# The DMAs of the row of maxima, issued by ScalarE in place of SyncE, in a two-layer attention kernel

## The chip, the cores and the metric

The kernel runs on one core of a Trainium2 chip. The metric is the device time of one execution in microseconds (us); lower is better. PE is TensorE, ACT is ScalarE, DVE is VectorE, POOL is GpSimd, SP is SyncE.

## The reference

Two blocks, each attention followed by a feed-forward layer, over x of shape (2, 2048, 256), 16 heads of 16, all in float32:

```
x = x + attn_a(layernorm(x))     # softmax(q k^T / 4, causal), then times a decay matrix of width 512, then v, then W_proj
x = x + ffn(layernorm(x))        # weights are sign(w) times a mean of |w|; gelu between
x = x + attn_b(layernorm(x))     # plain causal softmax attention with biases, and a norm behind it
x = x + ffn(layernorm(x))        # same ffn weights
```

The softmax subtracts the maximum of each query's scores. That maximum is what the change is about.

## The kernel before

The program is a chain of phases: `setup`, then for each of the two layers `projections`, `attention`, `output_projection` and `feed_forward`. `attention` runs twice, as `att_a` (with decay) and as `att_b` (without). In it the 2 × 16 heads are worked off in 8 groups of 4 heads (`GH`), and the 2048 queries of a head in 4 chunks (`c`) of 512 (`CH`).

Each group needs two passes over the scores. The first, items `M` of the plan, computes scores with queries on the partitions (PE, line 841, PSUM tile `pm`) and DVE takes the maximum of each row (lines 776 and 780, tile `mpart`). When a chunk is done (`MF`, `mneg`), PE turns the 16 columns of maxima into rows (`MT`, line 848, tile `px`), and DVE copies them to `mrow` (line 813). The item `MC` then brings `mrow`, 4 DMAs of 2 KB for each chunk, into row 64 (`MROW`) of the query operand `qop`. The second pass, items `S`, computes scores with keys on the partitions (PE, line 867, PSUM tile `ps`). Row 64 of `kop` is one, so the product already has the maximum subtracted, and ACT takes the exponential straight from PSUM (line 739, tile `wt`). The items `PV` and `PO` multiply `wt` with the values (lines 892, 902) and with ones (line 885). In att_a POOL multiplies `wt` by the decay first (line 700, tile `wd`), and for keys that are too far away for the decay table to be non-zero only their share of the sum is needed: ACT takes an exponential in the first pass' own PSUM tile (`FX`, line 746), and the items `FE` (ACT, line 753), `FM` (DVE, line 799), `FT` (PE, line 854) and `FC` (DVE, SP) make a total of them.

`attention_plan` writes down one order of all these items for a step. Every engine walks the same list and does its own part of each item, so the order on an engine's queue is the order of the plan. The first pass runs ahead of the second: in one step of the plan the second pass of group g stands with chunks 2 and 3 of the first pass of group g (d = 0) and chunks 0 and 1 of group g + 1 (d = 1). So a steady step has four `MC` items, the last step has two, and a list ahead of the first step has two. `S` of a chunk starts with a wait of PE for that chunk's `MC` DMAs:

```
if kb == near(c, decayed)[0] and j == 0:
    pe.wait_ge(m_in[c], M_DMAS * (g + 2))
```

PSUM has 4 banks for `pm` and 2 for `ps` in att_a, and 3 and 3 in att_b. PE's n-th `S` waits until ACT's exponential of 2 (or 3) `S` items before is done.

SP's queue has, in the order of the plan, the `MC` DMAs, the DMAs of `FC`, the stores of `y` (`O`), and at the end of a step `load(g + 2)`: 36 DMAs of keys and queries and one of 1 MB of values, 5 MB in all. Before the first step it has both `load(0)` and `load(1)`. SP waits before each `MC` until DVE has written `mrow` (semaphore `x_read`). In the plan `MC` stands between two `S` items, and in chunk 3 of att_a just ahead of `FE`.

Of the kernel before, what the change touches and what calls it, by code (L numbers as in the profile page):

```python
# [9 lines left out]
F32 = mybir.dt.float32  # L10
# [9 lines left out]
CH = 512  # L20
NC = T // CH
TB = CH // P
GH = 4
# [9 lines left out]
MROW = PAIRS * HD  # L33
# [408 lines left out]
def near(c, decayed):  # L442

    return range(TB * max(0, c - 1) if decayed else 0, TB * (c + 1))


def far(c, decayed):

    return range(max(0, c - 1) if decayed else 0)
# [86 lines left out]
def attention(nc, name, decayed, keep, dram):  # L536
# [3 lines left out]
    with ExitStack() as ctx:  # L540
# [4 lines left out]
        qop = sb("qop", [P, 2, GH, T], F32R)  # L545
# [7 lines left out]
        mrow = sb("mrow", [UNITS, NC, P], F32R)  # L553
# [9 lines left out]
        m_in = [sm(f"m_in{c}") for c in range(NC)]  # L563
# [3 lines left out]
        x_written, x_read, mrow_ready = sm("x_written"), sm("x_read"), sm("mrow_ready")  # L567
# [22 lines left out]
        def steps(eng, step):  # L590


            step(-1, -1, 1, FIRST)
            for g in range(GROUPS - 1):
                step(g, g // 2, g % 2, STEP)
            step(GROUPS - 1, GROUPS // 2 - 1, 1, LAST)

        def x_use(g, c, of_sums):

            return X_USES * g + c + sum(f < c for f in FARS) + of_sums  # L600
# [22 lines left out]
        def maxima(g, i, par, d):  # L623

            return (par, i) if d == 0 else (1 - par, i + par)

        @block.sync
        def _(sp):
            for i in range(2):
                sp.sem_inc(y_out[i], 16)  # L630
            for c in range(NC):
                sp.sem_inc(m_in[c], M_DMAS)
            for c in FARS:
                sp.sem_inc(f_out[c], 16)

            def load(g, par, first):
                for c in range(NC):
                    cols = slice(c * CH, (c + 1) * CH)
                    for r in range(PAIRS):
                        rows = slice(r * HD, (r + 1) * HD)  # L640

                        sp.dma_start(kop[rows, par, :, cols].bitcast(F32), qk_g[g, r % 2, 1, :, :, cols]).then_inc(qk_in[par][c], 16)
                        sp.dma_start(qop[rows, par, :, cols].bitcast(F32), qk_g[g, r // 2, 0, :, :, cols]).then_inc(qk_in[par][c], 16)
                    if first:
                        sp.wait_ge(q_padded[par], c + 1)
                    sp.dma_start(qop[MROW:MROW + 1, par, :, cols].bitcast(F32),
                                 qop[96:97, par, :, cols].bitcast(F32)).then_inc(qk_in[par][c], 16)
                sp.dma_start(va[:, par, :, :, :].rearrange("p (c t) j e -> p c (t j e)", c=NC), v_g[g])\
                  .then_inc(v_in[par], 16)

            def step(g, i, par, plan):
                for item in plan:
                    if item[0] == "MC":
                        _, d, c = item
                        mpar, _ = maxima(g, i, par, d)
                        sp.wait_ge(x_read, x_use(g + d, c, 0) + 2)
                        for j in range(GH):
                            sp.dma_start(qop[MROW:MROW + 1, mpar, j, c * CH:(c + 1) * CH].bitcast(F32),
                                         mrow[TB * j:TB * j + TB, c, :].bitcast(F32)).then_inc(m_in[c], 16)
                    if item[0] == "FC":  # L660
                        _, d, c = item
                        sp.wait_ge(x_read, x_use(g + d, c, 1) + 2)
                        sp.dma_start(far_g[g + d, c], frow[:, FARS.index(c), :]).then_inc(f_out[c], 16)
                    if item[0] == "O":
                        c = item[1]
                        sp.wait_ge(o_kept, NC * g + c + 2)
                        sp.dma_start(y_g[g, c], y[:, c % 2, :]).then_inc(y_out[c % 2], 16)
                if plan is STEP and g < GROUPS - 2:

                    sp.wait_ge(e_scores, E_UNITS * (g + 1))  # L670
                    sp.wait_ge(pv_done, KBS * (g + 1) + buffers)
                    load(g + 2, par, False)

            load(0, 0, True)
            load(1, 1, True)
            steps(sp, step)
            for i in range(2):
                sp.wait_ge(y_out[i], 16 * (GROUPS * NC // 2 + 1))
            for c in FARS:
                sp.wait_ge(f_out[c], 16 * (GROUPS + 1))  # L680
# [42 lines left out]
        @block.scalar  # L723
        def _(act):
            act.sem_inc(e_weights, EBANKS)
            act.sem_inc(o_kept, 1)
            act.sem_inc(f_done, MBANKS)

            def step(g, i, par, plan):
                seen = 0  # L730
                for item in plan:
                    if item[0] == "S":
                        _, c, kb, j = item
                        a = P * max(0, kb - TB * c)
                        kq = seen // GH
                        act.wait_ge(e_scores, E_UNITS * g + seen + 1)

                        act.wait_ge(pv_done, KBS * g + kq + 1)
                        act.activation(wt[:, kq % buffers, j, a:CH], pe_[:, seen % EBANKS, 0:CH - a], ACT.Exp)\  # L739
                           .then_inc(e_weights, 1)  # L740
                        seen += 1
                    if item[0] == "FX":
                        _, d, n, c, qb, j, piece = item
                        act.wait_ge(m_reduced, M_UNITS * (g + d) + n + 1 + MBANKS)
                        u = TB * j + qb
                        act.activation(pm[:, n % MBANKS, :], pm[:, n % MBANKS, :], ACT.Exp,  # L746
                                       bias=mpart[:, c, piece, u:u + 1],
                                       accum_out=fsum[:, c, piece, u:u + 1]).then_inc(f_done, 1)
                    if item[0] == "FE":
                        _, d, c = item  # L750
                        act.wait_ge(f_diff, len(FARS) * (g + d) + FARS.index(c) + 1)
                        n = len(far(c, decayed))
                        act.activation(ffactor[:, c, 0:n, :], ffactor[:, c, 0:n, :], ACT.Exp).then_inc(f_factor, 1)
                    if item[0] == "O":
                        c = item[1]
                        act.wait_ge(pv_done, KBS * g + sum(len(near(a, decayed)) for a in range(c + 1)) + buffers)
                        act.wait_ge(y_out[c % 2], 16 * (2 * g + c // 2 + 1))
                        act.activation(y[:, c % 2, :], po[:, :], ACT.Copy).then_inc(o_kept, 1)  # L758

            steps(act, step)  # L760

        @block.vector
# [720 lines left out]
```

## Time and profile before

| what | value |
|---|---|
| three runs | 3030.36, 3037.56, 3042.88 us; median 3037.56 |
| the profiled execution | 3037.05 us, span 3035.3 us |
| busy: PE, DVE, ACT, POOL | 2530.0, 1994.2, 1551.7, 922.8 us |
| mean granted clock of PE | 0.916 of full speed |
| att_a, att_b | from about 164 to 1230 us and from about 1658 to 2725 us of the span |
| SP's queue (q1), ACT's queue (q10) | 223.36 MB and 16.78 MB |

The span is from the first to the last instruction; the time of the execution has 1.75 us around it. "Busy" leaves out waits and also the instructions that issue DMAs. Rows of a timeline give start, duration, engine, line, operation, what is written and read, the count, and in brackets the idle time before and what ended it. A row whose engine is SPq or ACTq is work of that engine's instruction queue.

### The profile page before, as it was taken

Reading aid. Unit: us, or ns where it says so; the run is one execution under the profiler, and the core shown is the slowest. Engines: PE = TensorE matmul, PEld = TensorE weight load, DVE = VectorE, ACT = ScalarE, POOL = GpSimd, SP = SyncE. Lnnn points to the kernel's source line nnn. Section 1 sums busy time; section 2 is a strip of 40 time slices with the busy share of each in tenths; the row PEclk is TensorE's granted clock in tenths of the full one; section 3 lists DMA queues with packets and bytes.
Section 4 is the critical chain, followed back from the end, with each engine's and each line's share of the span. In section 5 each row is a group of like instructions: output and inputs, shape, how many; then the busy total and the mean of one; then the engine's idle time right before and its main releaser. Section 6 shows DMA issues by size and latency. Waiting matters only on the chain. (4 is left out here: it accounts for less than half of the span.)

```text
span 3035.3 us, 45097 instructions
## 1 busy us (share of the span) xinstructions
PE 2530.0 (83%) x14016; PEld 1465.7 (48%) x14016; DVE 1994.2 (66%) x4919; ACT 1551.7 (51%) x3394; POOL 922.8 (30%) x1108
## 2 busy tenths in 40 slices
PE   4847999999999999477975698989889898984498
PEld 3523545455454454356743354545445454533477
DVE  5555777777877775245654686768667686725755
ACT  1206676685776867114421065656556565660144
POOL 0025777777787778200001101011010110112100
PEclk8958999999999999778988599999999999997799
DMA  4992145052350500683269905052350513008632
GB/s 152 268 146 37 23 67 65 25 82 32 55 82 9 82 12 9 105 174 118 84 181 244 121 12 78 8 81 33 56 77 8 81 29 60 12 8 142 151 124 70
DMA packets 195001, 242.97 MB, mean 80 GB/s; under 512 B 25297, under 2 KB 119378, under 8 KB 194002
## 3 DMA queue, kind: packets, MB, share of 16 engines
q1 hardware_dynamic: 177874, 223.36, 39.2%
q10 hardware_dynamic: 16896, 16.78, 1.9%
q8 instruction: 114, 1.87, 0.3%
q14 instruction: 117, 0.96, 0.1%
HBM read 143.99 MB, written 95.03 MB: 79 GB/s over the span
## 5 line engine op out<-in xcount | busy, mean ns | idle before, releaser
L700 POOL TENSOR_TENSOR att_a_wd<-att_a_wt,decay 128x256 f32<-128x256 f32 (+3 forms) x896 | 754.4, 872 | 287.7 <-PE att_a_po L892 139.8
L739 ACT ACTIVATE att_b_wt<-att_b_ps 128x512 f32<-128x512 f32 (+3 forms) x1280 | 597.1, 538 | 443.2 <-PE att_b_ps L867 438.2
L776 DVE TENSOR_REDUCE att_a_mpart<-att_a_pm 128x1 f32<-128x512 f32 x768 | 509.6, 686 | 180.4 <-PE att_a_pm L841 178.4
L776 DVE TENSOR_REDUCE att_b_mpart<-att_b_pm 128x1 f32<-128x512 f32 x768 | 503.4, 686 | 172.3 <-PE att_b_pm L841 171.6
L739 ACT ACTIVATE att_a_wt<-att_a_ps 128x512 f32<-128x512 f32 (+3 forms) x896 | 437.0, 507 | 248.6 <-PE att_a_ps L870 170.7
L841 PE MATMUL att_a_pm<-att_a_kop,att_a_qop 128*128 128x512 f32 (+3 forms) x1280 | 511.0, 422 | 40.1 <-DMA att_a_qop<-att_a_qop 29.0
L867 PE MATMUL att_b_ps<-att_b_qop,att_b_kop 128*128 128x512 f32 (+3 forms) x1280 | 459.6, 389 | 93.9 <-DMA att_b_qop<-att_b_mrow 89.1
L841 PE MATMUL att_b_pm<-att_b_kop,att_b_qop 128*128 128x512 f32 (+3 forms) x1280 | 502.2, 412 | 28.4 <-DMA att_b_qop<-att_b_qop 27.9
L841 PEld LDWEIGHTS att_a_pm<-att_a_kop,att_a_qop 128*128 128x128 f32 x1280 | 239.2, 194 | 289.9 <-DVE att_a_mpart L776 117.4
L841 PEld LDWEIGHTS att_b_pm<-att_b_kop,att_b_qop 128*128 128x128 f32 x1280 | 249.7, 198 | 261.9 <-DVE att_b_mpart L776 107.8
L718 POOL TENSOR_SCALAR_AFFINE_SELECT att_b_wt<-att_b_wt 128x512 f32<-128x512 f32 x128 | 81.3, 635 | 963.1 <-ACT att_b_wt L739 963.1
L867 PE MATMUL att_a_ps<-att_a_qop,att_a_kop 128*128 128x512 f32 (+3 forms) x896 | 330.5, 376 | 37.9 <-DMA att_a_qop<-att_a_mrow 33.8
L867 PEld LDWEIGHTS att_b_ps<-att_b_qop,att_b_kop 128*128 128x128 f32 x1280 | 240.4, 192 | 206.1 <-DMA att_b_qop<-att_b_mrow 91.9
L780 DVE CUSTOM_DVE_ANT_0 att_b_pm<-att_b_pm,late 128x384 f32<-128x384 f32 (+3 forms) x512 | 247.6, 498 | 99.6 <-PE att_b_pm L841 97.4
L902 PE MATMUL att_b_po<-att_b_wt,att_b_va 128*32 128x512 f32 (+3 forms) x2560 | 301.1, 542 | 8.5 <-ACT att_b_y L758 7.8
L746 ACT ACTIVATE att_a_pm<-att_a_pm,att_a_mpart 128x512 f32<-128x512 f32 x384 | 255.1, 666 | 92.6 <-DVE att_a_mpart L776 91.2
L780 DVE CUSTOM_DVE_ANT_0 att_a_pm<-att_a_pm,late 128x384 f32<-128x384 f32 (+3 forms) x512 | 249.5, 497 | 55.6 <-PE att_a_pm L841 54.3
L867 PEld LDWEIGHTS att_a_ps<-att_a_qop,att_a_kop 128*128 128x128 f32 x896 | 169.6, 190 | 119.4 <-ACT att_a_wt L739 51.1
L885 PE MATMUL att_a_po<-att_a_wt,ones_strip 128*32 128x512 f32 (+3 forms) x1792 | 199.1, 513 | 13.6 <-ACT att_a_y L758 13.6
L892 PE MATMUL att_a_po<-att_a_wd,att_a_va 128*32 128x256 f32 (+3 forms) x1792 | 167.1, 445 | 3.7 <-POOL att_a_wd L700 3.7
L1066 PE MATMUL out_b_pp<-out_b_wp,out_b_yn 128*128 128x256 f32 x256 | 72.6, 453 | 68.5 <-DVE out_b_yn L1135 42.9
L1066 PE MATMUL out_a_pp<-out_a_wp,out_a_yn 128*128 128x256 f32 x256 | 78.3, 480 | 59.0 <-DVE out_a_yn L1135 59.0
(189 smaller groups left out, 2632.9 us busy)
## 6 DMA issues: line engine op xcount, KB each, us to landing
att_a_kop<-qk SPq DMA_DIRECT2D x128, 128.0 KB
att_a_qop<-qk SPq DMA_DIRECT2D x128, 128.0 KB
att_b_kop<-qk SPq DMA_DIRECT2D x128, 128.0 KB
att_b_qop<-qk SPq DMA_DIRECT2D x128, 128.0 KB
qk<-qkv_a_qk_hi SPq DMA_DIRECT2D x32, 256.0 KB, 4.9
qk<-qkv_a_qk_lo SPq DMA_DIRECT2D x32, 256.0 KB, 4.3
v<-qkv_a_vt SPq DMA_DIRECT2D x32, 256.0 KB, 4.0
att_a_va<-v SPq DMA_DIRECT2D x8, 1024.0 KB, 22.5
```

The source lines that it names most:

```text
L700: pool.tensor_tensor(wd[:, kq % 2, j, a:z], wt[:, kq % buffers, j, a:z], keep["decay"][:, u:u + z - a], ALU.mult).then_inc(w_decayed, 1)
L718: pool.affine_select(out=block, in_=block, compare_op=ALU.is_ge, fill=0.0, base=0, pattern=[[0, GH], [1, P]], channel_multiplier=-1).then_ ...
L739: act.activation(wt[:, kq % buffers, j, a:CH], pe_[:, seen % EBANKS, 0:CH - a], ACT.Exp)\
L746: act.activation(pm[:, n % MBANKS, :], pm[:, n % MBANKS, :], ACT.Exp, bias=mpart[:, c, piece, u:u + 1], accum_out=fsum[:, c, piece, u:u + ...
L776: dve.tensor_reduce(mpart[:, c, piece, u:u + 1], pm[:, n % MBANKS, 0:w], AX.X, ALU.max, negate=True).then_inc(m_reduced, 1)
L780: dve.tensor_tensor_reduce(out=pm[:, n % MBANKS, 0:w], in0=pm[:, n % MBANKS, 0:w], in1=keep["late"][:, CH - w:CH], scale=-1.0, scalar=-2 * ...
L841: mm = pe.matmul(pm[:, bank, 0:w], qop[:, mpar, j, q0:q0 + P], kop[:, mpar, j, piece * CH:piece * CH + w], start=True, stop=True)
L867: mm = pe.matmul(pe_[:, bank, 0:CH - a], kop[:, par, j, kb * P:(kb + 1) * P], qop[:, par, j, c * CH + a:(c + 1) * CH], start=True, stop=no ...
L885: mm = pe.matmul(po[STRIP * j:STRIP * (j + 1), a:CH], keep["ones_strip"][:, :], wt[:, ones % buffers, j, a:CH], start=first, stop=False)
L892: mm = pe.matmul(po[STRIP * j:STRIP * (j + 1), a:z], va[:, par, kb, j, :], wd[:, kq % 2, j, a:z], start=False, stop=last)
L902: mm = pe.matmul(po[STRIP * j:STRIP * (j + 1), a:CH], va[:, par, kb, j, :], wt[:, kq % buffers, j, a:CH], start=first, stop=last)
L1066: mm = pe.matmul(pp[:, par, t, :], yn[:, par, g, t * P:(t + 1) * P], wp[:, g, :], start=(g == 0), stop=(g == NG - 1))
```

## The change

The four DMAs of `MC`, with the wait for `x_read` ahead of them, go from the list of SP to that of ACT. They keep their place in the plan, their data and their semaphore. ACT's queue has its own DMA queue (q10). Nothing else is changed.

```diff
@@ attention, block.sync, step
-                    if item[0] == "MC":
-                        _, d, c = item
-                        mpar, _ = maxima(g, i, par, d)
-                        sp.wait_ge(x_read, x_use(g + d, c, 0) + 2)
-                        for j in range(GH):
-                            sp.dma_start(qop[MROW:MROW + 1, mpar, j, c * CH:(c + 1) * CH].bitcast(F32),
-                                         mrow[TB * j:TB * j + TB, c, :].bitcast(F32)).then_inc(m_in[c], 16)
@@ attention, block.scalar, step, between "S" and "FX"
+                    if item[0] == "MC":
+                        _, d, c = item
+                        mpar, _ = maxima(g, i, par, d)
+                        act.wait_ge(x_read, x_use(g + d, c, 0) + 2)
+                        for j in range(GH):
+                            act.dma_start(qop[MROW:MROW + 1, mpar, j, c * CH:(c + 1) * CH].bitcast(F32),
+                                          mrow[TB * j:TB * j + TB, c, :].bitcast(F32)).then_inc(m_in[c], 16)
```

## Rows read from the trace of the kernel before

**Rows 1.** Busy time by stretch, a group of att_b: us, engines, clock, DMA, GB/s.

```profile
1739.00:1878.00 139.00, 136.96 (x778) 72.99 (x777) 110.27 (x274) 92.74 (x200) 12.71 (x20) 0.98 0.19 28
```

**Rows 2.** Waits of PE in att_a, in att_b, then its first wait there.

```profile
PE att_a_ps L867 <- DMA att_a_qop<-att_a_mrow: 33.8, 1, 33.8
...
PE att_b_ps L867 <- DMA att_b_qop<-att_b_mrow: 63.2, 7, 12.0
...
1737.32 0.79 PE L867 MATMUL att_b_ps<-att_b_qop,att_b_kop 128*128 128x512 f32 x1 [25.95 <-DMA att_b_qop<-att_b_mrow]
```

**Rows 3.** Timeline of SP's queue behind a load in att_b.

```profile
1876.68 2.84 SPq L658 DMA_DIRECT2D att_b_qop<-att_b_mrow  x4
```

**Rows 4.** Busy time by stretch, around one wait in att_b.

```profile
1885.00:1898.00 13.00, 1.00 (x10) 0.33 (x2) 1.28 (x2) 0.00 (x0) 0.63 (x1) 0.69 0.93 162
...
1900.00:1902.00 2.00, 2.00 (x12) 0.97 (x11) 1.14 (x2) 1.19 (x2) 0.00 (x0) 0.50 0.00 0
```

**Rows 5.** Instructions by line: count, ns min/median/max, first and last start.

```profile
L658 SPq DMA_DIRECT2D att_b_qop<-att_b_mrow x128: 572/573/6400, 1710.4 to 2681.0; - x128
...
L1085 ACTq MOVE x<-out_b_xo x8: 29/29/29, 2769.4 to 2872.2; - x8
L1085 ACTq DMA_DIRECT2D x<-out_b_xo x8: 378/379/410, 2769.5 to 2872.3; - x8
...
L1215 SPq DMA_DIRECT2D out<-ffn_b_xo x8: 384/384/384, 2914.1 to 3031.4; - x8
```

**Rows 6.** DMA queues and issues from 2769 to 2785 us.

```profile
q1 hardware_dynamic: 1449, 1.64, 64.5%
...
x<-out_b_xo ACTq DMA_DIRECT2D x1, 512.0 KB, 4.3
```

**Rows 7.** Instructions of line 648, the load of values.

```profile
L648 SPq DMA_DIRECT2D att_b_va<-v x8: 442/442/1231, 1676.0 to 2508.8; - x8
...
DMA to landing us min/median/max: 18.9/22.3/27.4
```

**Rows 8.** att_a, chunks 2 and 3: timelines of SP, PE, ACT; line 746 in all.

```profile
398.49 2.45 SPq L658 DMA_DIRECT2D att_a_qop<-att_a_mrow  x4
...
400.61 0.39 PE L867 MATMUL att_a_ps<-att_a_qop,att_a_kop 128*128 128x512 f32 x1
...
445.19 0.23 ACT L753 ACTIVATE att_a_ffactor<-att_a_ffactor 128x32 f32<-128x32 f32 x1 [1.57 <-DVE att_a_ffactor L792]
...
446.62 0.39 PE L854 MATMUL att_a_px<-ident,att_a_ftotal 128*16 128x128 f32 x2 [1.06 <-DVE att_a_ftotal L802]
...
L746 ACT ACTIVATE att_a_pm<-att_a_pm,att_a_mpart 128x512 f32<-128x512 f32 x384 | 255.1, 666 | 92.6 <-DVE att_a_mpart L776 91.2
```

**Rows 9.** att_a, chunk 0 of the next group: timelines of SP and PE.

```profile
462.31 2.42 SPq L658 DMA_DIRECT2D att_a_qop<-att_a_mrow  x4
...
463.94 0.40 PE L867 MATMUL att_a_ps<-att_a_qop,att_a_kop 128*128 128x512 f32 x1
```

**Rows 10.** att_b, chunk 2: timelines of ACT and PE.

```profile
1875.60 2.48 ACT L739 ACTIVATE att_b_wt<-att_b_ps 128x512 f32<-128x512 f32 x4 [0.86 <-PE att_b_ps L867]
...
1879.13 0.34 PE L867 MATMUL att_b_ps<-att_b_qop,att_b_kop 128*128 128x384 f32 x1
```

**Rows 11.** att_b, chunks 3 and 1: timelines of SP and PE.

```profile
1931.13 2.42 SPq L658 DMA_DIRECT2D att_b_qop<-att_b_mrow  x4
...
1931.78 0.34 PE L867 MATMUL att_b_ps<-att_b_qop,att_b_kop 128*128 128x256 f32 x1
...
1966.38 2.42 SPq L658 DMA_DIRECT2D att_b_qop<-att_b_mrow  x4
...
1967.53 0.45 PE L867 MATMUL att_b_ps<-att_b_qop,att_b_kop 128*128 128x512 f32 x1
```

**Rows 12.** Busy time by stretch at chunk 3 in att_a.

```profile
692.00:695.00 3.00, 1.50 (x12) 1.01 (x16) 2.11 (x6) 0.86 (x3) 1.08 (x1) 1.00 0.00 1
695.00:698.00 3.00, 3.00 (x15) 1.77 (x10) 1.24 (x9) 0.73 (x2) 1.53 (x2) 0.57 0.02 5
```

## The prediction, made before the result was known

> **What bounds the kernel now.** I read the windows first, then the waits of PE, then the timelines around those waits. In the steady part of an attention phase PE is the bound: it is busy 136.96 of 139 us at a granted clock of 0.98, while ACT has 92.74 and DVE 110.27 [rows 1]. Its queue is in order, so whatever holds its next instruction is added to the end. The waits of PE name one transfer that does so: the row of maxima (`mrow` into `qop`), 33.8 us once in att_a, 26.0 us once at the start of att_b (ended at 1737.32), and 63.2 us in seven waits later in att_b, up to 12.0 us each [rows 2]. The reader is to see that the row is tiny (2 KB) and its DMAs late for what stands ahead of them. In a steady group of att_b SP issues them at 1876.68 [rows 3], just behind a group's load of 5 MB. During the wait that follows, from 1885 to 1898, PE does 1.00 us of work while the DMA engines are at 0.93 [rows 4]. The row lands when the load has drained. At the start SP issues the first rows only at 1710.4 [rows 5], after both first loads.
>
> **What the change gives.** On ACT's queue the row is not behind the load in SP's ring. Whether the same 16 engines then serve it early is shown by the out_b stage: there ACT's queue stored 512 KB with a landing of 4.3 us in a stretch where SP's queue used 64.5% of the engines [rows 6]. Here the row has from 1876.68 to the wait at about 1886, 9 us, for 2 KB. I take all six long waits as gone. By the Trainium skill (DMA: Bandwidth & Descriptors, Queues, rings and completion order) each DMA engine takes turns between the queues that have work, a packet at a time; the stretch of out_b agrees, and with strict order the 63.2 would stay.
> At the start the next hold would be the values of V: issued at 1676.0, landing in 18.9 to 27.4 us [rows 7], so by 1703.4; PE's wait in att_b began at 1737.32 − 25.95 = 1711.4 [rows 2]. So both start waits go whole. Gain in waits: 33.8 + 26.0 + 63.2 = 123.0 us.
> After a long wait PE restarts slowly: at 1900 to 1902 the granted clock is still 0.50 [rows 4], that is 1.2 of 2.4 GHz. PE restarted at about 1898 and was at half clock some 5 us, a loss of 2.5. Six such waits: 15 us. The start has low clock before its waits too, so I give nothing there. Gain in all: **138 us**.
>
> **What it costs: the issue itself.** SP's DMA of a row takes 573 ns, and four of them 2.42 us with the gaps [rows 5, 8]. On SP that time was free. ACT's queue is also the one that starts the exponentials, so each `MC` now holds the next exponential by 2.42 us plus a wait for DVE's copy. A 512 KB store costs 379 ns on ACT and 384 on SP, but on ACT a MOVE of 29 ns stands ahead of each [rows 5]. I take 2.55 us for four; the bounds are 1.5 (four at 379) and 2.75 (four with a move and a register instruction of some 50 more).
> Behind it in ACT's order is the exponential that frees a PSUM bank of `ps`, and PE's `S` matmul two banks (att_a) or three (att_b) later waits for that. So the stall of PE is: start of the issue, + 2.42, + the exponential, less the time at which PE ran that matmul before. For the eight places, one group of each:
> - att_a, chunk 2: two `FX` exponentials of 0.67 stand between too. 398.49 + 2.42 + 1.34 + 0.6 = 402.85, against 400.61: 2.3 us [rows 8].
> - att_a, chunk 3: PE itself waits for a chain that begins with ACT's `FE`, started at 445.19. `MC` stands ahead of `FE`, so `FE`, DVE's product and PE's matmul at 446.62 slide by the issue and the 0.2 us to the copy: 2.6 [rows 8].
> - att_a, chunks 0 and 1 of the next group: 462.31 + 2.42 + 0.6 = 465.33, against 463.94: 1.4 each [rows 9].
> - att_b, chunk 2: the issue begins after the second exponential of the four from 1875.60, about 1876.2; + 2.42 + 0.6 = 1879.3, against 1879.13: 0.2 [rows 10].
> - att_b, chunk 3: 1931.13 + 2.42 + 0.4 = 1933.95, against 1931.78: 2.2 [rows 11].
> - att_b, chunks 0 and 1: 1966.38 + 2.42 + 0.6 = 1969.40, against 1967.53: 1.9 each [rows 11].
>
> That is 7.7 us a group in att_a and 6.2 in att_b, seven groups each, and 4.9 and 2.4 for the last, which has no next group: 58.8 + 45.8 = 104.6 us. The 0.13 us by which I put the four above 2.42 adds 8 over 60 places. At the start of att_a ACT's second issue also delays `FX` work: 2. Hidden costs: SP's queue is only relieved, and ACT's own busy time has room (92.74 of 139, [rows 1]); it's the order, not the sum, that hurts. I count a stall whole, because PE has no slack to win it back.
>
> **What it costs: the clock.** In one group of att_a PE was busy 1.50 of 3 us at the chunk-3 place and the granted clock then read 0.57 for the next 3 us [rows 12]. The dip costs 3 × 0.43 = 1.3 us. The change adds 2 to 3 us of idle time just where PE already waits. I count 26 dips (the 16 chunk-3 places, the 8 of att_a's chunk 2, 2 others) at 1.3: 34 us. Bounds: 0, and one at every place, 60 × 1.3 = 78. Cost in all: 104.6 + 8 + 2 + 34 = **149 us**.
>
> The sum: 149 − 138 = +11 us on the profiled execution's own 3037.05 (span 3035.3), which lies 0.5 under the median of the three runs, 3037.56. **3048 us.**
>
> **Rivals.**
> - *The issue is mostly hidden (faster).* ACT waits for PE once a round of four exponentials, 0.86 us in [rows 10], and if the DMA instructions go by at 1.5 us for four, each stall is 0.9 shorter: 52 left of 105. With few dips (10 us) the cost is 64, and the time 3037 − 138 + 64 = 2963; with half of that relief about 3005. It decides if four issues on ACT take under some 2 us. Against it: the row's DMA took 573, not 379, wherever it was seen.
> - *The row still lands behind the load (slower).* Then only the issue moves: the 63.2 and 15 stay, and perhaps the start too: 3037 + 149 = 3186 at worst, 3126 if the start is still won. For it speaks that all engines were at 0.93 and more; against it [rows 6]. A sentence of the Trainium skill (Trainium Kernel Development and Optimization, Key Constraints) says that issuing from several engines saves only the sequencer's issue time. Read strictly it would make this rival the result, since here the sequencer's time is what gets dearer.
> - *The clock drops at every new stall (slower).* 78 in place of 34: 3092; with four issues of 2.75 us, 12 more, 3104.
> - *Another transfer holds the start (slower).* If V or the zeroing of the row is the last in at both starts, up to 59.8 of gain goes: 3108.
>
> **How the numbers follow.** My likeliest case, both terms near their estimates (3020 to 3078), has 0.52: of it 0.27 lies within 0.5% (15 us, about what a measurement of this kernel can tell from no change) and 0.25 above. Faster, the issue mostly hidden, has 0.27, at 2963 to 3020. The clock rival has 0.11, the row behind the load 0.06, another transfer at the start 0.04; all slower. So faster 0.27, same 0.27, slower 0.46. The range leaves out the deeper half of the first rival and the two worst: 2985 to 3105. The likeliest case's own range is 3020 to 3078.
>
> **What would show it.** The waits of PE should name `mrow` nowhere for more than 1 us, and the start of att_b should have no gap of 26 us. ACT's queue should show 256 row DMAs; their time, 573 ns or not, settles the first rival at once. PE should wait for ACT's exponentials for some 80 us, and at the `FT` matmul 2.6 us more in each of eight places. Granted clock: the six long dips of att_b gone, short ones at chunk 3 in their place. I am wrong if the ACT rows are short, if PE's new waits are under 1 us a place, or if the wait for `mrow` at chunk 2 of att_b stays.

## The result, and the profile after

| | before | after |
|---|---|---|
| median | 3035.86 us (4 runs, 3030.36 to 3042.88) | 3087.86 us (4 runs, 3086.34 to 3089.5) |
| profiled execution, span | 3037.05, 3035.3 | 3087.32, 3085.6 |
| mean granted clock | 0.916 | 0.913 |
| PE busy, PE not busy (span less busy) | 2530.0, 505.3 | 2587.1, 498.5 |

The ratio is 1.017, with a 95% interval of 1.0148 to 1.0193: the changed kernel is 1.7% slower. The forecast was 3048, 0.4% above before; the time lies inside its range of 2985 to 3105, and above the likeliest case's own range, which ended at 3078.

The last line of the table is the shortest account of it. PE has 6.8 us less of idle time than before and 57.1 us more of busy time, for the same 14016 matmuls. So the waits that were won and the waits that were added nearly cancel, and what is left over is slower work. The page of the profile after:

```profile
PE 2587.1 (84%) x14016; PEld 1488.5 (48%) x14016; DVE 1997.2 (65%) x4919; ACT 1548.3 (50%) x3394; POOL 922.9 (30%) x1108
...
q1 hardware_dynamic: 175826, 222.83, 38.5%
q10 hardware_dynamic: 18944, 17.31, 1.9%
```

ACT's queue (q10) has grown from 16.78 to 17.31 MB: the 256 rows have moved. Their issues, by line:

```profile
L740 ACTq DMA_DIRECT2D att_a_qop<-att_a_mrow x128: 580/580/1197, 189.4 to 1246.3; - x128
L740 ACTq DMA_DIRECT2D att_b_qop<-att_b_mrow x128: 580/580/760, 1746.3 to 2727.2; - x128
```

One takes 580 ns on ACT, as against 573 on SP [rows 5], and not 379. Next the waits of PE (releaser: total us, times, longest). Beside those for the row [rows 2], the kernel before had these, the first three in att_a:

```profile
PE att_a_px L854 <- DVE att_a_ftotal L802: 9.8, 8, 1.5
PE att_a_pm L841 <- ACT att_a_pm L746: 6.8, 17, 0.5
PE att_a_ps L867 <- ACT att_a_wt L739: 3.9, 7, 0.6
...
PE att_b_ps L867 <- ACT att_b_wt L739: 3.4, 15, 0.2
```

The changed kernel has these:

```profile
PE att_a_pm L841 <- ACT att_a_pm L746: 28.5, 26, 2.6
PE att_a_px L854 <- DVE att_a_ftotal L802: 27.7, 8, 4.2
PE att_a_ps L867 <- ACT att_a_wt L732: 25.4, 22, 1.6
...
PE att_b_ps L867 <- ACT att_b_wt L732: 53.5, 43, 2.8
PE att_b_ps L867 <- DMA att_b_qop<-att_b_mrow: 7.4, 4, 2.2
```

The waits for the row went from 33.8 + 26.0 + 63.2 = 123.0 us to 7.4. Those for ACT (directly, or through the chain that ACT's `FE` begins) went from 23.9 to 135.1, so by 111.2. Together: −4.4 of the −6.8.

A steady group of att_a shows what is left. The windows before and after hold the same stretch of the plan, one whole group (us, busy PE, PEld, DVE, ACT, POOL, clock, DMA, GB/s). Before:

```profile
391.02:513.58 122.56, 116.99 (x791) 61.49 (x791) 96.07 (x241) 86.75 (x213) 94.33 (x112) 1.00 0.35 52
```

After:

```profile
369.77:505.62 135.85, 123.02 (x788) 64.35 (x787) 95.58 (x241) 86.61 (x212) 94.17 (x112) 0.95 0.32 47
```

The group of att_a is 13.3 us longer: 7.3 of it is idle time of PE (12.83 against 5.57), 6.0 is PE's work at 0.95 of the clock in place of 1.00. DVE and POOL have the same busy time as before: nothing else got dearer.

### The profile page after: what moved, and what is told of

The parts are those of the page before. It is cut to its first block and busy times, and to the rows that moved or that the text cites. A ratio compares the mean times of both kernels' runs of the same rounds, so it can differ in the third digit from the quotient of the medians.

```text
span 3085.6 us, 45097 instructions
## 1 busy us (share of the span) xinstructions
PE 2587.1 (84%) x14016; PEld 1488.5 (48%) x14016; DVE 1997.2 (65%) x4919; ACT 1548.3 (50%) x3394; POOL 922.9 (30%) x1108
## 3 DMA queue, kind: packets, MB, share of 16 engines
q10 hardware_dynamic: 18944, 17.31, 1.9%
## 5 line engine op out<-in xcount | busy, mean ns | idle before, releaser
L841 PE MATMUL att_a_pm<-att_a_kop,att_a_qop 128*128 128x512 f32 (+3 forms) x1280 | 522.9, 433 | 60.7 <-DMA att_a_qop<-att_a_qop 29.1
L841 PEld LDWEIGHTS att_a_pm<-att_a_kop,att_a_qop 128*128 128x128 f32 x1280 | 247.6, 201 | 323.3 <-DVE att_a_mpart L776 122.3
L841 PEld LDWEIGHTS att_b_pm<-att_b_kop,att_b_qop 128*128 128x128 f32 x1280 | 253.2, 200 | 260.4 <-DVE att_b_mpart L776 104.6
L711 POOL TENSOR_SCALAR_AFFINE_SELECT att_b_wt<-att_b_wt 128x512 f32<-128x512 f32 x128 | 81.2, 635 | 949.3 <-ACT att_b_wt L732 949.3
L867 PE MATMUL att_a_ps<-att_a_qop,att_a_kop 128*128 128x512 f32 (+3 forms) x896 | 338.4, 385 | 25.5 <-ACT att_a_wt L732 25.4
L902 PE MATMUL att_b_po<-att_b_wt,att_b_va 128*32 128x512 f32 (+3 forms) x2560 | 309.8, 557 | 8.6 <-ACT att_b_y L758 7.9
L885 PE MATMUL att_a_po<-att_a_wt,ones_strip 128*32 128x512 f32 (+3 forms) x1792 | 204.6, 525 | 13.3 <-ACT att_a_y L758 13.3
L892 PE MATMUL att_a_po<-att_a_wd,att_a_va 128*32 128x256 f32 (+3 forms) x1792 | 175.4, 465 | 3.7 <-POOL att_a_wd L693 3.7
```

The lines of the kernel that those rows point to most:

```text
L711: pool.affine_select(out=block, in_=block, compare_op=ALU.is_ge, fill=0.0, base=0, pattern=[[0, GH], [1, P]], channel_multiplier=-1).then_ ...
L841: mm = pe.matmul(pm[:, bank, 0:w], qop[:, mpar, j, q0:q0 + P], kop[:, mpar, j, piece * CH:piece * CH + w], start=True, stop=True)
L867: mm = pe.matmul(pe_[:, bank, 0:CH - a], kop[:, par, j, kb * P:(kb + 1) * P], qop[:, par, j, c * CH + a:(c + 1) * CH], start=True, stop=no ...
L885: mm = pe.matmul(po[STRIP * j:STRIP * (j + 1), a:CH], keep["ones_strip"][:, :], wt[:, ones % buffers, j, a:CH], start=first, stop=False)
L892: mm = pe.matmul(po[STRIP * j:STRIP * (j + 1), a:z], va[:, par, kb, j, :], wd[:, kq % 2, j, a:z], start=False, stop=last)
L902: mm = pe.matmul(po[STRIP * j:STRIP * (j + 1), a:CH], va[:, par, kb, j, :], wt[:, kq % buffers, j, a:CH], start=first, stop=last)
```

## The experiments

All ratios are to the kernel before, run beside on the same chip, with 95% intervals. "Waits for ACT" adds the four rows shown above. "PE busy" is from the profiled execution; the kernel before has 2530.0, and waits for ACT of 23.9.

| kernel | what ACT does at each `MC` | median us | ratio | waits for ACT | PE busy |
|---|---|---|---|---|---|
| wait_only | waits, issues nothing | 3037.35 | 0.999 (0.9975 to 1.0004) | 25.1 | 2531.6 |
| issue_only | issues 4, no wait | 3034.74 | 0.999 (0.9977 to 1.0002) | 24.9 | 2529.4 |
| issue_long | issues 8, no wait | 3116.25 | 1.0262 (1.0241 to 1.0282) | 88.8 | 2560.4 |
| issue4_wait | waits, then issues 4 | 3147.0 | 1.0374 (1.0349 to 1.0399) | 93.3 | 2568.3 |
| issue6_wait | waits, then issues 6 | 3251.7 | 1.0718 (1.0692 to 1.0744) | 163.1 | 2611.7 |
| issue_long_wait | waits, then issues 8 | 3335.91 | 1.1004 (1.0974 to 1.1035) | 212.6 | 2650.2 |
| start_only | rows ahead of the first step alone | 2969.72 | 0.9787 (0.9765 to 0.9808) | 25.9 | 2519.2 |
| where_late | those and att_b's chunk 2 | 2931.15 | 0.9645 (0.9619 to 0.9672) | 37.5 | 2520.5 |
| one_dma | all rows, one DMA for four | 2923.38 | 0.9619 (0.9592 to 0.9645) | 31.9 | 2518.8 |
| where_late_one | where_late and one_dma | 2907.58 | 0.9582 (0.9566 to 0.9599) | 22.6 | 2511.1 |
| one_dma_sp | nothing (SP, one DMA for four) | 3027.44 | 0.9974 (0.9962 to 0.9986) | 22.9 | 2523.2 |

In the first six of these the row itself stays on SP. In the five of them that issue, ACT's DMAs write 2 KB each of a constant to a buffer in DRAM that nobody reads, and ACT waits for them once, at the end of a phase. That is work added to the kernel before, so each shows a cost without the gain. The cuts of code below leave out such lines and what follows from a new layout; `...` marks the place.

**Is it the wait or the issue?** wait_only adds ACT's wait and nothing else; issue_only adds four DMAs and no wait.

```diff
 wait_only
+                    if item[0] == "MC":
+                        _, d, c = item
+                        act.wait_ge(x_read, x_use(g + d, c, 0) + 2)
 issue_only
+                    if item[0] == "MC":
+                        _, d, c = item
+                        for j in range(GH):
+                            act.dma_start(spare[g + d, c, j:j + 1, :], keep["decay"][0:TB, 0:P]).then_inc(spare_out, 16)
...
```

> The kernel before, with ACT waiting for x_read at each place of MC and issuing nothing; SP still issues the row. If the issue is what costs, this changes under 15 us (ACT is 0 to 1 us early at most places and waits for PE anyway): 3030 to 3050. If ACT's wait for DVE is what costs, most of the cost is here: over 3100.

> The kernel before, with four extra DMAs of 2 KB on ACT's queue at each place of MC (a constant tile to spare DRAM, 256 DMAs in all), and no wait ahead of them; the row of maxima still goes by SP, so nothing is gained. If the four issues (2.44 us on ACT in the changed kernel) are what costs, the waits of PE for ACT's exponentials and for the FT chain grow by 60 to 100 us over both attention phases, more short stretches of half clock appear, and the time is 3110 to 3190. It is a little less than the changed kernel's whole cost, because an issue without the wait for x_read starts up to 1.6 us earlier at chunk 3. If the wait for DVE's copy is what costs, the time stays within 15 us of before. If it is the traffic on a second queue, the DMAs' landings get longer and PE's waits are for DMAs.

Neither cost anything. wait_only came as expected; issue_only missed its 3110 to 3190 altogether. ACT's queue in issue_only shows why:

```profile
389.43 0.61 ACT L740 ACTIVATE att_a_wt<-att_a_ps 128x512 f32<-128x512 f32 x1
389.49 0.59 ACTq L746 DMA_DIRECT2D spare_a<-decay  x2
389.91 0.62 ACT L740 ACTIVATE att_a_wt<-att_a_ps 128x512 f32<-128x512 f32 x1
390.11 0.67 ACTq L746 DMA_DIRECT2D spare_a<-decay  x2
390.82 0.66 ACT L751 ACTIVATE att_a_pm<-att_a_pm,att_a_mpart 128x512 f32<-128x512 f32 x1 [0.30 <-issue]
```

The reader is to see that the four DMAs go out from 389.49 to 390.78 while two exponentials already handed to ACT run until 390.53; ACT itself stands still for 0.30 us. It is also a short issue: four take 1.29 us here, not 2.44. So it was no copy of the change, for two reasons, length and place, and neither result alone could be taken as the cost of a part.

**Length.** issue_long is issue_only with `range(2 * GH)`, 3.3 us of issue.

> As issue_only, but eight extra DMAs at each place in place of four: the four took ACT's queue only 1.28 us, where the four rows take it 2.44, so that run did not have the suspected length. Eight take about 2.6 us, still with no wait ahead. If the time of the issue costs once it is longer than what ACT has in hand at a place (two or three exponentials already dispatched, and banks of PSUM in reserve), PE's waits for ACT and for FT rise by 30 to 80 us over before, short stretches of half clock appear, and the time is 3070 to 3140. If length does not matter, it stays at 3037 within 15. SP's queue and the row are as before.

It cost 2.6%, within what was expected, with 88.8 us of waits for ACT. So an issue without a wait costs too once it is long; by the timeline of issue_only I take the exponentials started ahead of it as the measure of "long", which no run tests alone.

**The wait ahead of the issue.** issue_long_wait, issue6_wait and issue4_wait put wait_only's wait ahead of 8, 6 and 4 DMAs.

```diff
+                        act.wait_ge(x_read, x_use(g + d, c, 0) + 2)
+                        for j in range(4):
+                            act.dma_start(spare[g + d, c, j:j + 1, :], keep["decay"][0:TB, 0:P]).then_inc(spare_out, 16)
...
```

> issue_long with ACT's wait for x_read ahead of the eight DMAs: the whole of what the change puts on ACT (2.6 us where the change has 2.44), and none of what it gives. If the change is the sum of a gain of about 115 to 125 us and a cost, this run shows the cost alone: 3037 + 170 = 3207, range 3160 to 3240, with PE's waits for ACT and FT up by about 110 us and 60 to 90 us of half clock in att_a. If the changed kernel's cost had come from the row's DMAs themselves (their traffic, their landing), this run is under 3100.

> Six extra DMAs at each place on ACT, after the wait for x_read; SP issues the row. In issue_long_wait the eight held ACT's queue 3.8 us and not 2.6, so that run overstated the change's burden (299 us). Six should take about 2.6 us (four take 1.28, each further one some 0.6), close to the 2.44 of the change. If the change is this burden less a gain of about 120 us, this run is 3037 + 170, range 3180 to 3240. If it is under 3120, the changed kernel lost time in another way than by the hold of ACT's queue.

> Four extra DMAs after the wait for x_read, held 1.28 us. With no wait the same four cost nothing (0.999), and the wait with nothing behind it cost nothing either. If an issue behind the wait can't hide behind exponentials already dispatched, the two together cost: ACT's next exponential is 0.6 to 1.3 us late, against about 1 us that the PSUM banks give PE; FT in att_a waits 1.3 us more in 8 places. 3050 to 3085. If the two effects only add, it stays at 3037 within 10.

issue4_wait is the one that tells most: of two parts that each cost nothing, the sum costs 3.7%, and the 3147 us lie above the 3050 to 3085 that I had expected. One of its issues, in the timeline of ACT:

```profile
455.58 1.90 ACTq L747 DMA_DIRECT2D spare_a<-decay  x4
```

Its waits of PE, over both phases:

```profile
PE att_b_ps L874 <- ACT att_b_wt L740: 33.3, 43, 2.2
PE att_a_pm L848 <- ACT att_a_pm L752: 21.6, 26, 2.1
PE att_a_px L861 <- DVE att_a_ftotal L809: 21.1, 8, 3.6
PE att_a_ps L874 <- ACT att_a_wt L740: 17.3, 21, 1.1
```

The same four DMAs now take 1.90 us, and they begin when the wait ends. By then the exponentials ahead of them have run, so they have no cover. (That the cover is what makes the difference is how I read the two timelines; the runs show that wait and issue together cost, and apart don't.)

With no issue, and with 1.90, 3.12 and 3.8 us of it (medians over the places) behind the wait, the time over before is 0 (wait_only), 111, 215 and 299 us. Between 1.90 and 3.12, the change's 2.44 us come to 111 + 0.54/1.22 × 104 = 157 us. issue_long_wait missed its expectation (3160 to 3240) with 3336, because its hold was 3.8 us, not the 2.6 I had assumed from issue_only. issue6_wait missed its own (3180 to 3240) with 3252 in the same way: its six took 3.12 us, not 2.6.

**The gain by itself.** start_only leaves all rows on SP but those ahead of the first step; where_late also moves att_b's chunk 2.

```diff
 start_only
+        def on_act(g, item):
+
+            return g < 0
...
 where_late
+            return g < 0 or (not decayed and item[1:] == (0, 2))
...
 both, in the steps of ACT and of SP
+                    if item[0] == "MC" and on_act(g, item):
+                    if item[0] == "MC" and not on_act(g, item):
...
```

> Only the four rows ahead of the first step (two in each phase) go by ACT, four DMAs each, where ACT has nothing else to do; all others on SP. PE's first waits (33.8 and 26.0) go, the six at chunk 2 of att_b stay: 3037 - 60 = 2977, range 2965 to 2990, if both start waits are won whole. If V or a load holds PE instead, it is above 3005.

> Only those rows go by ACT that were late in the kernel before: the four ahead of the first step (both phases) and chunk 2 of each group of att_b, 12 of 64; all others stay on SP. If gain and cost are as I read them, the gain (waits of 115 us less the 7 that remain, and the long stretches of half clock in att_b) stays and the cost falls to some 8 stalls of 1.3 us: 2905 to 2945. If early landing is worth less than the waits it removes (another wait takes over), it is above 2980.

start_only gave 67 us, and as expected its one large wait for the row is the one in the steps of att_b:

```profile
PE att_b_ps L878 <- DMA att_b_qop<-att_b_mrow: 62.1, 7, 11.2
```

where_late gave 108 us; its waits for the row are 12.2 us in all, those for ACT in att_b 14.1, which is 10.7 more than before for its eight places there. Both came inside what was expected.

**The issue made short.** one_dma keeps the change but lays `qop` out so that the four heads' rows of a chunk are one run of 8 KB, and issues one DMA.

```diff
-        qop = sb("qop", [P, 2, GH, T], F32R)
+        qop = sb("qop", [P, 2, NC, GH, CH], F32R)
...
-                        for j in range(GH):
-                            act.dma_start(qop[MROW:MROW + 1, mpar, j, c * CH:(c + 1) * CH].bitcast(F32),
-                                          mrow[TB * j:TB * j + TB, c, :].bitcast(F32)).then_inc(m_in[c], 16)
+                        act.dma_start(qop[MROW:MROW + 1, mpar, c, :, :].bitcast(F32),
+                                      mrow[:, c, :].bitcast(F32)).then_inc(m_in[c], 16)
...
```

> The changed kernel with the query operand laid out by chunk, so that the row of a chunk (8 KB) goes by one DMA on ACT in place of four. If the length of the issue is what costs, one issue of about 0.6 us holds ACT by a quarter as long: PE's waits for ACT fall from about 107 us to under 40, the half clock in att_a falls from about 78 us to under 30, and the time is 2920 to 2970, well below the kernel before. If the place in ACT's order (the wait for x_read) is what costs, the time stays above 3050. A third case: one DMA of 16 pieces takes four times as long to issue; then it is near 3088.

Its issues by line, for att_a:

```profile
L740 ACTq DMA_DIRECT2D att_a_qop<-att_a_mrow x32: 510/526/640, 186.7 to 1161.3; - x32
```

Its waits of PE in att_a and in att_b:

```profile
PE att_a_px L854 <- DVE att_a_ftotal L802: 14.7, 8, 2.3
PE att_a_pm L841 <- ACT att_a_pm L746: 6.8, 17, 0.5
PE att_a_ps L867 <- ACT att_a_wt L733: 4.6, 8, 0.6
...
PE att_b_ps L867 <- DMA att_b_qop<-att_b_mrow: 8.5, 6, 2.1
PE att_b_ps L867 <- ACT att_b_wt L733: 5.8, 22, 0.9
```

The wait is as before and the place too; only the hold is 0.53 us instead of 2.44. The waits for the row are down to 8.5 us and nearly all of those added for ACT are gone with them, and the kernel is 3.8% faster, inside what was expected. one_dma_sp is the control: the new layout and the one DMA, on SP.

> The kernel before (SP issues the row) with the query operand laid out by chunk and one DMA of 8 KB for a row. The control for one_dma: if the new layout or the smaller number of DMAs gave its 115 us by themselves, this is near 2923; if the early landing did, the waits for mrow stay at 115 to 123 us and the time is 3020 to 3040.

It gained 0.3%, with its waits for the row still 30.4 and 86.1 us. So of one_dma's 115 us some 10 come from layout and count, and the other 104 from the queue.

**Both.** where_late_one has one_dma's layout and where_late's choice. Its waits of PE in att_b stand under the expectation.

> one_dma and where_late together: one DMA for a row, on ACT only ahead of the first step and at chunk 2 of att_b, all others on SP. What one_dma still pays at the other places (5 us more at FT in att_a, 2 at the exponentials of att_b, little clock) goes: 2905 to 2923. If the places on ACT cost nothing any more with one DMA, it is the same as one_dma within 5 us.

```profile
PE att_b_ps L877 <- DMA att_b_qop<-att_b_mrow: 7.9, 6, 1.8
PE att_b_ps L877 <- ACT att_b_wt L743: 3.4, 15, 0.2
```

Every wait for ACT is back where the kernel before had it, and the time is 2907.58 us, the fastest here: 4.2% under before. Against start_only and where_late it says that the move was worth its price at 12 of its 64 places (4 ahead of the first steps, 8 in att_b), and with four DMAs not at the other 52.

## Why the prediction was right or wrong

The time lies 40 us above the 3048. Both sums of waits came within 8 us of the forecast. The term that was mis-sized is the clock's cost: 34 us were laid down for it, and about 63 were measured.

**The waits won: right, 123 forecast, 115.6 measured.** The two long waits at the starts are gone. The second pass of att_a begins at 214.69 in place of 246.52; here are the first `S` of both phases after, neither with a wait:

```profile
214.69 0.63 PE L867 MATMUL att_a_ps<-att_a_qop,att_a_kop 128*128 128x512 f32 x1
...
1775.49 0.63 PE L867 MATMUL att_b_ps<-att_b_qop,att_b_kop 128*128 128x512 f32 x1
```

In the steps the waits for the row do not quite vanish: four are left, the longest 2.2 us, where the prediction said that none would be over 1 us. One place in att_b, chunk 2, on ACT's queue and on PE:

```profile
1920.17 2.44 ACTq L740 DMA_DIRECT2D att_b_qop<-att_b_mrow  x4
1923.37 0.50 PE L867 MATMUL att_b_ps<-att_b_qop,att_b_kop 128*128 128x512 f32 x1 [1.33 <-ACT att_b_wt L732]
1934.43 0.50 PE L867 MATMUL att_b_ps<-att_b_qop,att_b_kop 128*128 128x512 f32 x1 [1.12 <-DMA att_b_qop<-att_b_mrow]
...
1968.48 0.58 PE L867 MATMUL att_b_ps<-att_b_qop,att_b_kop 128*128 128x256 f32 x1 [2.18 <-ACT att_b_wt L732]
1986.62 0.50 PE L867 MATMUL att_b_ps<-att_b_qop,att_b_kop 128*128 128x512 f32 x1 [1.16 <-ACT att_b_wt L732]
```

The last of the four was issued by 1922.6, and PE went on at 1934.43, 12 us later, while the load on SP's queue filled the engines (their share reads 1.08 in the window from 1922 to 1934). The estimate had allowed 9 us and called it enough, from a landing of 4.3 us in a stretch where SP's queue used 64.5%; another store of the same size on ACT's queue in that stretch took 10.7. The Trainium skill (DMA: Bandwidth & Descriptors, Queues, rings and completion order) says that an engine takes turns between queues packet by packet; the runs agree in direction, since 63.2 us of waits became 7.4, but not as if the row went first. The rival in which the row still lands behind the load is out. So is, as a forecast for this kernel, the strict reading of the Trainium skill's sentence (Trainium Kernel Development and Optimization, Key Constraints) that a second issuing engine saves only issue time: in one_dma it made issuing dearer for ACT and the kernel 115 us faster, 104 us of it against the same layout on SP.

**The waits added: right, 104.6 us forecast (and 10 of small terms), 111.2 measured.** By place, from the groups shown: att_a chunk 2, 2.35 (forecast 2.3); chunk 3, 3.03 at the `FT` matmul against 1.06 before, so 2.0 (2.6; over all eight groups 2.2); chunks 0 and 1, 1.40 and 1.58 (1.4 each). att_b chunk 2, 1.33 (0.2); chunk 3, 2.18 (2.2); chunks 0 and 1, 1.16 and 1.88 (1.9 each). The chunk 2 of att_b was the place that the estimate had too cheap: it took the issue to begin after the second of four exponentials already started. Two of the prediction's differences are rounded up (402.85 − 400.61 is 2.24, 1879.22 − 1879.13 is 0.09), which is worth 1.4 us over all groups. Its upper bound of 2.75 us for an issue counts some 50 ns for a register instruction, which no run shows; four took 2.44. The first of the two att_a places, as the timeline after shows it:

```profile
377.27 2.44 ACTq L740 DMA_DIRECT2D att_a_qop<-att_a_mrow  x4
379.75 0.66 ACT L746 ACTIVATE att_a_pm<-att_a_pm,att_a_mpart 128x512 f32<-128x512 f32 x1 [3.07 <-issue]
380.67 0.47 PE L841 MATMUL att_a_pm<-att_a_kop,att_a_qop 128*128 128x512 f32 x1 [2.35 <-ACT att_a_pm L746]
```

ACT stands 3.07 us for the issue, its next exponential is late, and PE waits 2.35 us for the bank that this exponential frees. It is PSUM tile `pm` that PE waits for here, not `ps` as the step had it; the size came out the same.

**The clock: the term that was mis-sized, 34 us forecast, about 63 measured.** PE's busy time rose by 57.1 us. Here it is by stretch, where the "steps" of a phase run from its first `S` matmul to its last matmul:

| PE busy, PE not busy (us) | before | after | where_late_one |
|---|---|---|---|
| steps of att_a | 932.2, 49.8 | 966.4, 108.0 | 930.5, 48.4 |
| steps of att_b | 905.8, 81.2 | 923.4, 75.5 | 894.5, 26.6 |
| all the rest | 692.0, 374.3 | 697.3, 315.0 | 686.1, 317.6 |

The windows behind it: before (att_a, att_b), after (the same), and where_late_one in att_b.

```profile
246.52:1228.50 981.98, 932.23 (x6297) 487.24 (x6297) 739.33 (x1819) 693.32 (x1700) 754.40 (x896) 1.00 0.28 42
1737.32:2724.30 986.98, 905.76 (x5102) 474.70 (x5102) 695.08 (x1732) 610.51 (x1312) 81.34 (x128) 0.96 0.27 42
...
214.69:1289.10 1074.41, 966.38 (x6298) 500.12 (x6296) 739.03 (x1823) 693.60 (x1702) 754.24 (x896) 0.96 0.28 42
1775.49:2774.40 998.91, 923.38 (x5103) 479.68 (x5102) 700.60 (x1736) 607.33 (x1312) 81.24 (x128) 0.96 0.29 45
...
1672.70:2593.80 921.10, 894.49 (x5103) 466.42 (x5102) 694.86 (x1736) 608.79 (x1312) 81.23 (x128) 1.00 0.32 48
```

In att_a's steps no row was late, so their 34.1 us are cost alone, as much as the prediction had laid down for both phases. In att_b's steps where_late_one has the gain without the added waits for ACT: 11.3 us of busy time less than before (the prediction said 15). The changed kernel has 28.9 more than that, which is the cost there. In the rest the kernels do the same work, and the 5.3 us are put down to nothing in the change: the other kernels, whose work is the same there, read 685.8 to 695.1. So 34.1 + 28.9 − 11.3 + 5.3 gives the 57. Without the gain, issue4_wait (1.90 us) has 39.8 us more busy time than before in the steps of both phases, and issue6_wait (3.12) 80.9; between them 2.44 us come to 58, near the 63.

Why 63 and not 34? At a place of chunk 2 and one of chunk 3 in att_a, then at a place of chunk 0 there, in windows of after:

```profile
377.00:382.00 5.00, 2.65 (x17) 1.01 (x13) 1.88 (x6) 2.25 (x7) 1.38 (x2) 0.92 1.09 122
382.00:385.00 3.00, 3.00 (x14) 1.88 (x14) 1.95 (x5) 2.67 (x7) 2.75 (x3) 0.56 1.08 128
...
427.00:432.00 5.00, 1.97 (x16) 0.92 (x8) 1.58 (x6) 0.61 (x2) 1.87 (x2) 1.00 0.01 2
432.00:435.00 3.00, 3.00 (x15) 1.41 (x15) 1.21 (x8) 0.49 (x1) 0.95 (x1) 0.57 0.03 8
435.00:436.00 1.00, 1.00 (x6) 0.95 (x5) 0.59 (x3) 0.49 (x1) 1.00 (x3) 0.59 0.00 0
...
452.50:459.50 7.00, 6.33 (x27) 3.06 (x26) 3.65 (x10) 2.46 (x5) 2.86 (x4) 0.53 0.12 41
```

After a stall of 2.35 or 3.03 us PE works at 0.56 or 0.57, nearly the lower of the two levels (1.2 of 2.4 GHz). That is the dip of the prediction [rows 12]. But the prediction's window of 3 us ended before that dip did. The next one of before reads

```profile
698.00:699.00 1.00, 1.00 (x8) 0.65 (x10) 0.91 (x5) 0.49 (x1) 1.00 (x2) 0.59 0.00 0
```

so that dip cost 1.7 us and not 1.3. And some dips of after are twice as long: at 452.5 the clock stays low for 7 us, beside a stall of only 1.40 us and one of 0.67. Windows of 0.5 us over the steps show 32 stretches of low clock in the changed kernel (19 in att_a, 13 in att_b, without the one that each phase's steps begin in), 21 of them of 3.5 to 4 us and 11 of 7 to 7.5. They stand at 15 of the 16 chunk-3 places, at 7 of att_a's 8 chunk-2 places, and ten times elsewhere (two of these at waits for the row). So the count of 26 was nearly right, place by place. The size of a dip was wrong: 63 us over 32 are 2.0 us each. Why some are twice as long as others no run here shows.

The rival that the clock falls at every new stall (78 in place of 34: 3092 us, or 3104) is the nearest to the measured 3088 by its number, but not by its mechanism: about half of the new stalls had no dip.

One gap stays open. By whole times, the cost without the gain (157 us at 2.44) less the gain without the cost (130, where_late_one) leaves +27, less where_late's 108 it leaves +49, and +52 was measured. Part of it can be argued: in issue4_wait and issue6_wait PE still waits for the row at att_b's chunk 2, so an issue on ACT costs little there, where where_late shows 10.7 us of added waits. The rest may lie in the interpolation.

**The rival "mostly hidden" was decided by its own point,** four issues under 2 us. They took 2.44. issue_only shows that its mechanism exists all the same: at 1.29 us and not behind a wait the issue is hidden whole.

## What to carry to other kernels

Count what an engine's queue holds, not its busy time: ACT had half its time free, and 2.44 us of DMA issue behind a wait cost PE 1.2 to 2.4 us at each place shown. Moving a small, urgent transfer off the queue that carries large loads is worth a lot (here 115.6 us of waits), so make the issue short (one DMA in place of four), and move only the places where the transfer was late. When a few long stalls are traded for many of 1 to 3 us with the same sum, look for a loss by the clock as well: here PE was busy 57 us longer for the same work. And when a dip of the clock is priced from a window, the window has to reach to the dip's end.

## What the runs showed of the hardware

- Two harmless parts, at 64 places each, made a dear whole: the wait alone 0.999, four issues alone 0.999, both 1.037.
- Issue cost depends on the transfer: 0.58 us for a 2 KB row within SBUF on ACT, 0.53 for one of 8 KB, so about a quarter of the cost for the same bytes. From SBUF to DRAM four took 1.29 us beside running exponentials and 1.90 behind a wait (median of one 0.32).
- A row's DMA on its own queue landed in 1.8 us where the engines were free, and in 12.9 to 13.9 at chunk 2 of att_b in six of the eight groups, beside a load of 5 MB on the other queue. The issues of one_dma, all 64:

```profile
DMA to landing us min/median/max: 1.8/1.8/13.9
```
